# First cross attention: where the value products stand inside a step of TensorE's program

## The reference, cut to what matters

```python
q = heads(x @ Wq + bq); k = heads(x @ Wk + bk); v = heads(x @ Wv + bv)
att = causal softmax(q k^T * scale)                 # 256 own keys
cq = heads(x @ Wcq + bcq); ck, cv = heads(ctx @ Wck + bck), heads(ctx @ Wcv + bcv)
catt = softmax(cq ck^T * scale)                     # 1601 context keys
y = (att @ v + catt @ cv) @ Wp + bp
```

## Time and profile before

| what | value |
|---|---|
| device time, median of 3 runs | 668.37 us (666.0 to 671.0) |
| device time of the profiled execution | 673.8 us |
| its span, first to last instruction | 672.0 us |
| mean granted TensorE clock | 0.963 of full speed |
| TensorE / VectorE / ScalarE busy | 613.4 / 514.0 / 449.2 us |
| main loop, first to last exponential | 84.5 to 372.1 us |

### The profile page before, as it was taken

How to read it: one execution, slowest core, us unless ns; L and a number is a source line. 1 busy time by engine, 2 the same in 40 slices (tenths; PEclk the granted TensorE clock), 3 DMA queues, 4 the chain that set the end, 5 groups by cost and what they waited for, 6 DMA issues and landing times. The chain is left out here.

```text
span 672.0 us, 13625 instructions
## 1 busy us (share of the span) xinstructions
PE 613.4 (91%) x5208; PEld 339.5 (51%) x5210; DVE 514.0 (76%) x704; ACT 449.2 (67%) x818; POOL 220.3 (33%) x299
## 2 busy tenths in 40 slices
PE   8979998999999989999999689899719899999996
PEld 5644543444444434444433367688304556657884
DVE  5358996999999989999970349799589767786632
ACT  3555586999999979999999345455782156666224
POOL 8214433243644557767668203000000000014000
PEclk9999997999999999999999969899968999999999
DMA  8257596656656554445411036884000010000000
GB/s 215 96 150 227 180 269 151 151 145 165 156 122 168 132 136 93 94 87 117 101 46 40 17 96 219 315 316 158 1 0 0 5 43 1 2 1 0 1 0 32
DMA packets 44799, 71.39 MB, mean 106 GB/s; under 512 B 13252, under 2 KB 32764, under 8 KB 44352
## 3 DMA queue, kind: packets, MB, share of 16 engines
q1 hardware_dynamic: 31840, 38.34, 21.8%
q0 software_dynamic: 12288, 29.95, 14.6%
q10 hardware_dynamic: 608, 2.25, 1.5%
HBM read 44.94 MB, written 24.81 MB: 104 GB/s over the span
## 5 line engine op out<-in xcount | busy, mean ns | idle before, releaser
L1000 ACT ACTIVATE prob<-ps 128x512 f32<-128x512 f32 (+2 forms) x480 | 251.0, 583 | 30.8 <-PE ps L767 22.8
L1124 DVE TENSOR_REDUCE pm<-ps 128x2 f32<-128x1024 f32 x192 | 224.3, 1209 | 8.6 <-PE ps L725 8.4
L767 PE MATMUL ps<-qq,kc 50*128 50x256 bf16 (+1 forms) x832 | 134.3, 276 | 5.6 <-DMA qq<-mrow 5.6
L790 PE MATMUL ps<-prob,vst 128*9 128x256 f32 (+1 forms) x1664 | 132.2, 383 | 2.8 <-ACT o_all L988 2.8
L725 PE MATMUL ps<-kc,qq 48*128 48x512 bf16 x384 | 118.8, 389 | 1.9 <-DVE pm L1124 1.2
L767 PEld LDWEIGHTS ps<-qq,kc 50*128 50x128 bf16 (+1 forms) x832 | 52.9, 96 | 102.6 <-ACT prob L1000 80.8
L790 PEld LDWEIGHTS ps<-prob,vst 128*9 128x9 f32 (+1 forms) x1664 | 27.7, 88 | 44.4 <-ACT prob L1000 28.4
L713 PE MATMUL ps<-masks_b 64*128 64x256 bf16 x256 | 38.3, 271 | 0.0
L725 PEld LDWEIGHTS ps<-kc,qq 48*128 48x128 bf16 x384 | 34.1, 94 | 8.2 <-DVE pm L1124 3.6
L1460 ACT ACTIVATE sg<-ps,exp_bias 128x512 f32<-128x512 f32 x32 | 21.9, 685 | 21.9 <-PE ps L1376 21.9
L1131 DVE TENSOR_REDUCE nm<-ps 128x4 f32<-128x512 f32 (+1 forms) x32 | 30.6, 957 | 7.6 <-PE ps L713 6.4
(11 more groups left out here) (367 smaller groups left out, 1293.2 us busy)
## 6 DMA issues: line engine op xcount, KB each, us to landing
kc<-kc_scr SPq DMA_DIRECT2D x32, 300.2 KB, 4.8
below<-rden_scr POOLq DMA_DIRECT2D x15, 256.0 KB, 5.9
comb_bc<-comb_scr SPq DMA_DIRECT2D x7, 512.0 KB, 4.4
ctx<-ctx_scr POOLq DMA_DIRECT2D x4, 801.0 KB, 6.6
raw<-in_wexp POOLq DMA_DIRECT2D x8, 384.0 KB, 3.6
exp_scr<-raw_high POOLq DMA_DIRECT2D x8, 384.0 KB, 2.7
exp_scr<-raw_low POOLq DMA_DIRECT2D x8, 384.0 KB, 3.8
kc_scr<-hi SPq DMA_DIRECT2D x6, 400.2 KB, 4.0
```

The lines of the kernel that those rows point to most:

```text
L767: last = pe.matmul(bank[0:p, j * TQ:(j + 1) * TQ], kc[s][rows, j, t * 128:t * 128 + p], qq[s][rows, 0, j, :], start=(j == 0), stop=True, s ...
L790: last = pe.matmul(o_ps[32 * hh:32 * hh + VW, kind * TQ + q0:(kind + 1) * TQ], value[:, hh * VW:(hh + 1) * VW], prob[0:k, (NST * n + t) % ...
L1000: act.activation(prob[0:p, g % P_RING, 2 * e:2 * e + 2, q0:TQ], s2[0:p, k % S2_RING, 0:2 * w].rearrange("p (i q) -> p i q", i=2), ACT.Exp, ...
L1124: dve.tensor_reduce(pm[:, m % 2, c, :, jt], banks, AX.X, ALU.max).then_inc(s1_read, 1)
```

## The change

`scores_and_half` gets one more argument, the step whose value products it is to issue, and issues them between the two score pairs of its step. Before, the main loop issued them after all score products of the step. Which step's value products they are (two steps back), what they wait for and what they compute stay the same. The last two steps' value products behind the loop stay where they were, and so do the first two steps, in which idle products stand in their place.

```diff
-                    def scores_and_half(g, h):
+                    def scores_and_half(g, h, between=None):
...
                         scores_t(n, t, 0, 0)
                         if more:
                             score_wait(m, i)
                             score_part(m, i, 1)
                         scores_t(n, t, 0, 1)
+                        if between is not None:
+                            outputs(between // NST, between % NST)
                         scores_t(n, t, 1, 0)
                         if more:
                             last = score_part(m, i, 0)
...
                     for g in range(NU * NST):
                         n, t = g // NST, g % NST
-                        scores_and_half(g, g + HALVES + S1_LEAD)
-                        if g >= 2:
-                            outputs((g - 2) // NST, (g - 2) % NST)
-                        else:
+                        scores_and_half(g, g + HALVES + S1_LEAD, g - 2 if g >= 2 else None)
+                        if g < 2:
                             if g:
                                 pe.wait_ge(exp_done, 2 * g)
                             keep_clock(2, 2 * (g + 1) % S2_RING)
```

## The result

| | before | after |
|---|---|---|
| device time, median | 669.7 us (4 runs) | 705.2 us (703.7 to 706.5, 4 runs) |
| ratio of the two | | 1.052, 95% interval 1.047 to 1.056 |
| span of the profiled execution | 672.0 us | 704.8 us |
| main loop, first to last exponential | 287.6 us | 324.2 us |
| mean granted TensorE clock | 0.963 | 0.977 |

The account below looks back on a forecast made before the run. Three nearly full engines bound the loop; splitting a half's parts lengthens its ring. 14.5 units times 2.4 us give plus 35, minus 2 given back: plus 33 on 668.4, 701 us, range 689 to 711, chance 0.82.

Parts of the forecast that it names:

- What bounds: Main loop before: TensorE, VectorE and ScalarE busy 17.30, 16.96 and 16.15 of 17.52 us a unit, none with room.
- TensorE's own work unchanged: Each step: same instructions, borders between scores and values, and row pairing, so TensorE's work stays 1.09 us.
- the turn: Products turning the maxima, once a unit: now ahead of scores, one more border of 0.09, 0.1 us a unit.
- the copy: A unit's first value products wait 0.4 us for ScalarE's copy out: 0.2 if one ring feels it, 0.4 if both.
- The half's ring: A half's first part to the first part two halves later: 2.57 us instead of 1.89, over two steps.
- Pieces 14, 13 and 12: Halves with masks, half-wide score products, and short stream with the turn behind: round trips of 2.99, 2.23 and 2.7 us.
- The unit: 15 steps of the main loop: half of 38.8 us plus smaller waits, 19.9 us, 2.4 above 17.52.
- the bound of 2.7: Upper bound on the loss per unit, in us, if every wait adds; the lower bound was 1.7.
- What it gives back: Two waits for DMAs bringing the maxima shrink by 1 us each: minus 2 us, at most minus 7 with clock loss.
- The clock didn't fall: Rival: TensorE's idling in each step lowers its clock once a unit, adding 15 us; about 716 us, chance 0.07.
- 668 and 665 us: Rivals: second part starts ahead of the value products, no change (0.06); ring has room, ScalarE fed more evenly, faster (0.03).
- the decisive time of 0.94 us: First part's start to second's end in a half: must stay below 0.94 us for the faster rival; forecast 1.25.

Follow-up runs that it names:

- e1: Changed kernel with both parts of the half ahead of the value products, which stay between the score pairs; 686.2 us, ratio 1.029 to the kernel before.
- e2: Changed kernel with both parts of the half behind the value products, which stay between the score pairs; 684.8 us, ratio 1.026 to the kernel before.
- e3: Changed kernel with value products between the score pairs only in even steps, behind the scores in odd ones; 695.7 us, ratio 1.042 to the kernel before.
- e5: Changed kernel with VectorE's wide reductions reading only 256 of 512 keys; 688.3 us, ratio 1.025 to the kernel before.
- e7: Changed kernel with ScalarE's copy out ahead of the exponential of step 1 instead of behind it; 701.0 us, ratio 1.046 to the kernel before.
- e8: Kernel before with the first pass 8 instead of 7 halves ahead; 672.7 us, ratio 1.004 to the kernel before.
- e9: Same as e8, with VectorE's reciprocal of the denominators also two halves later; 674.2 us, ratio 1.004 to the kernel before.
- e11: Same as e2, with the turn of the maxima moved to just ahead of the next step's value products; units of 18.34 us against 18.70 in e2.

## Why the prediction was right

I forecast 701 us (689 to 711) for the median before of 668.4; it is 705.2 against 669.7, so plus 35.5 where I had plus 33. By its steps:

- **What bounds.** Right. Three engines without room, and TensorE waits for a reduction by hundredths before; after, its weight loads wait 28 us in all.
- **TensorE's own work unchanged.** Right for ordinary steps: 1.10 us with the values in the middle in e1. Wrong for the others: with the parts kept together a unit is still 1.2 to 1.45 us longer (e1, e2). I had set 0.1 for the turn, as one more border, and 0.2 to 0.4 for the copy. The turn is 0.36 in e2: I had missed that its products ran beside the value products before, and that between the pairs they leave a pair of scores alone.
- **The half's ring.** Right, and for an undisturbed half to the hundredth: 2.58 us measured for 2.57 forecast, of it 1.27 us from the first part's start to the second's end (220.51 to 221.78) for 1.25. Pieces 14, 13 and 12 take 3.02, 2.29 and 2.91 for 2.99, 2.23 and 2.7. But only three wide halves in a unit take 2.58, and the mean of the twelve is 2.74. The sign "VectorE waiting ahead of nearly each wide reduction" came only in part: 58 of some 170 have a wait that the view shows. e3 and e5 show that it is the ring and not the place.
- **The unit.** Mis-sized: 20.53 us for 19.9, plus 3.01 for plus 2.4. My sum of the 15 rings was 38.8 us and it is 41.07, and even the bound of 2.7, "if every wait adds", lies too low. The copy's wait is 0.62 us for my 0.4, and its gain in e7 is whole (0.42 of 0.43) where I had counted 0.2 to 0.4. The rest is in the wide halves that take over 2.58 us, next to the turn, the copy and the short pieces, which I did not follow one by one.
- **What it gives back.** Mis-sized the other way. 14.5 units times 3.01 would be 43.6 us, and the loop grew by 36.6. The units that were held up by DMAs and the clock before (0, 1, 8 and 9: 79.4 us for four, 9.4 above 4 x 17.52) took 81.6 in the changed kernel, 0.5 below 4 x 20.53: minus 9.9. Against it stand 1.5 us of late DMAs in units 3 and 4 of the changed kernel and 1.1 in the last 22 steps, which I had left at nothing. I had minus 2, at most minus 7. In this trace the fall of the clock in the loop, granted 0.91 in unit 9, is gone too. Why exactly the DMAs are seldom late there is open: e8 and e9 gave them more time as well, and were held up all the same.
- **The rivals.** The ring binds, so 668 and 665 us are out; the decisive time of 0.94 us between the parts against the measured 1.27 was the right thing to look at. The clock didn't fall: granted 1.00 in all units of the loop, although TensorE's weight loads waited shortly for reductions some 70 times. The case told in the Trainium skill, page "TensorE: Matmul & The Clock Gate", section "A second HAM failure mode: psum-queue depth-cycling", did not come about here. The rule of the Trainium skill, same page, Part 3, that matmuls keep program order held for what mattered in the steps shown: the second part (221.39) started behind the value products (220.83).

The two errors, 0.6 us a unit too little (9 us over 14.5 units) and some 6 us too little given back, partly cancel. That the total is off by 2.5 us and not by 9 is luck. Of the 3.01 us a unit the runs give 1.6 to 1.8 to the ring and 0.4 to the copy's wait; the other 0.8 to 1.0 were not taken apart in the changed kernel itself.

## What to carry to other kernels

When work is moved into the middle of a step, list for each double buffer what lies between its first write and its release: the producing engine's own work can stay the same (1.09 us a step before, 1.10 in e1) and the loop still lengthen, because the buffer is held longer. Add up one trip round each ring (write, signal, read, release) and compare it with the number of buffers times the step; that sum was right to 0.01 us here for a half with nothing irregular beside it, and 0.17 too low in the mean of the twelve, so the irregular steps need to be followed one by one. And when two parts of one buffer must be split for packing, put nothing long between them. The same goes for products that run side by side on different rows: one that separates them cost 0.3 us each time here.

## What was not expected of the hardware

- The two products that turn the maxima cost 0.36 us a unit more between the pairs of scores than just ahead of the value products (e2 against e11), where the prediction had 0.1 and the expectation 0.2.
- The changed program, 3 us a unit slower, lost little to late DMAs and nothing in its loop to the clock (0.7 us in each of units 3 and 4, the others at the pattern), where the faster one lost 9.4 us. The traces of e1, e3, e5 and e7, with units of 18.97 to 20.23 us, also have a granted clock of 1.00 through the whole loop; every trace with shorter units has a unit at 0.92 or below in it. Giving the faster one a step more of lead moved its late places (units 11 and 13 in e8, five places in e9) instead of removing them.
